# Moving the tiles of a small attention to other SBUF columns, with a new merge of twelve streams of steps

## The chip, the cores and the metric

The kernel runs as one program on one core of a Trainium2 chip, in one launch. Its time is the device time of that core in microseconds (us). The kernel before took 1306.95, 1311.45 and 1311.14 us in three runs; the median is 1311.14 us.

## The reference

Four layers, each an attention and a feed-forward part, over 4 batches of 512 tokens with 128 features. What matters here is layer 0 and its experts, which fill the first third of the span:

```python
# layer 0 attention: 16 heads of 64, 4 key heads, a causal window of 64 tokens
q, k = rmsnorm(q, q_norm_w), rmsnorm(k, k_norm_w)
mask = (i >= j) & (i - j < WIN)
attn = softmax(where(mask, einsum("bhqd,bhkd->bhqk", q, k) / 8, -inf))
y = einsum("bhqk,bhkd->bqhd", attn, v) @ wo.T

# layer 0 feed-forward: a small attention over the 4 batches (at each token
# position, 16 heads of 8), then 8 experts of which each token takes 2
hn = layernorm(x);  q, k, v = split(hn @ in_proj_w.T + in_proj_b)
probs = softmax(where(causal, einsum("sbnd,tbnd->bnst", q, k) / sqrt(8), -inf))
x1 = x + einsum("bnst,tbnd->sbnd", probs, v) @ out_proj_w.T + out_proj_b
hn2 = layernorm(x1);  gates = top2(softmax(hn2 @ router_w.T))
out = x1 + einsum("tef,efh->th", gelu(einsum("th,ehf->tef", hn2, w1)) * gates, w2)
```

Layer 1 has a windowless causal attention (in two halves) and 8 gated experts, layer 2 an attention with 16 heads of 8 and a mixture of low-rank adapters, layer 3 a linear attention and a gated feed-forward.

## The kernel before

The kernel is written for the five engines directly, with semaphores. Its work is cut into 2593 steps. Twelve streams (named a to l) each hold a list of steps in a fixed order: a the layer norms, b the main attention, c the feed-forward, j the mix of layer 0's attention (softmax, transposes, values), l the projections, and so on. The string MERGE, counts and letters, says in which order steps are taken from the streams ("3cl" is three steps of c and one of l). That gives one list of steps for the whole program. Each step has a part on some of the engines, and each engine does its parts in the order of that list, strictly one after the other: a part that waits holds up all that stands behind it on its engine. A step that moves in the merge moves on every engine on which it has a part.

The steps that the change touches or that the prediction speaks of:

- The small attention across batches: `qkv0(b, k)` (ScalarE writes q, k or v of batch b), `bp`, `bs`, `bm`, `be`, `bd`, `bv`, `bo` (products, sums by head, exponentials, weighted sum), `bx` (projection and residual; x1 is left in the tile of k). Its tiles are called qkv; sc0 holds scores.
- Layer 0's attention, for each batch b: `q0(b, p)` and `k0(b, kv)` (projections, copied by VectorE to the arena, L1119 and after), `ks0(b)` (sums of squares, with a power by GpSimd, L1913, whose result TensorE's `kn0(b, kv)` turns), `sc(b, i, x)` (scores on TensorE, maximum by VectorE L1170, four exponentials by ScalarE L1709), `nz` (VectorE divides), `tp(b, i, x)` (transposes on TensorE, L432; copies to pbuf by VectorE L1191 and ScalarE L1721), `yv(b, i)` (values, TensorE), `yt` (L1728), `wo0` (output projection). Queries and keys of the even batches lie in arena columns 0 to 6399, those of the odd batches in columns 9728 to 16127.
- Experts of layer 0: `rts`, `dsp` (the routing), `xt(0, b)` (tokens turned, copied by ScalarE L1747 to tH, and scattered by GpSimd to slots_x in DRAM, 8 indirect DMAs for a batch, L1934). Then 39 blocks of 128 slots in ten groups: `xl(0, q)` (load wA<-slots_x, SyncE L1983; TensorE turns the blocks, L432, VectorE copies to xf, L1328), `up0(q, h)` (TensorE; ScalarE's gelu, L1756, in two halves), `dn0` (TensorE), `stored` (ScalarE's copy tH<-psB, L1764, then the store to slots_y, SyncE L1998), `wl(0, k)` (a block's weights, L1993). `cmb(0, b)` gathers the results from slots_y (GpSimd L1947) when all are stored.

On SyncE's queue the load of a later group (L1983) stands right behind the store of an earlier one (L1998). The tokens of a group sit in one of two buffers, in wA columns 3072 to 4095. The small attention and layer 0's attention share the arena:

```python
qsb = [av[:, o:o + 4096]... for o in (0, 9728)]
kk = [av[:, o + 4096:o + 6400]... for o in (0, 9728)]
qkv = av[:, 9728:15872]...
sc0 = av[:, 15872:18432]...
```

So batch 1's first queries could not be written before the small attention and the layer norm "h2", which reads x1, were done; `q0(1, 0)` waits for them on VectorE (4 waits on ln_xc, one on bo_done).

Of the kernel before, what the change touches and what calls it, by code (L numbers as in the profile page):

```python
# [11 lines left out]
ALU = mybir.AluOpType  # L12
ACT = mybir.ActivationFunctionType
# [38 lines left out]
    "ih3cich2ci2ci2cici5c")
# [108 lines left out]
def build(nc, d, out):  # L161
    ctx = ExitStack()
    with ctx:
# [10 lines left out]
        def cols(t, b):  # L174
            return t[:, b * T:(b + 1) * T]
# [92 lines left out]
        qkv = av[:, 9728:15872].rearrange("p (b a c) -> p b a c", b=4, a=3)  # L268
        sc0 = av[:, 15872:18432].rearrange("p (a c) -> p a c", a=5)
# [144 lines left out]
        def ln_src(tag, b):  # L414
            return qkv[:, b, 1, :] if tag == "h2" else cols(xn if tag == "h1" else xT, b)
# [10 lines left out]
        def tensor(pe):  # L426
# [579 lines left out]
        def vector(dv):  # L1006
# [85 lines left out]
            def bo(s):  # L1092
# [5 lines left out]
                dv.tensor_tensor(qkv[:, s, 0, :], sc0[:, 0, :], sc0[:, 4, :], ALU.mult).then_inc(*bo_done.up(s))  # L1098

            def bx(b):  # L1100
# [3 lines left out]
                dv.scalar_tensor_tensor(qkv[:, b, 1, :], misc("bx", b), vec("outb"), cols(xn, b), ALU.add, ALU.add) \  # L1104
# [3 lines left out]
                add_x(0, b, qkv[:, b, 1, :])  # L1108
# [1268 lines left out]
```

## Time and profile before

| | |
|---|---|
| runs | 1306.95, 1311.45, 1311.14 us; median 1311.14 |
| the profiled execution: time, span | 1302.39 us, 1300.6 us |
| instructions | 23823 |
| granted clock of TensorE, mean | 0.953 |
| busy share of PE, DVE, ACT, POOL | 91%, 69%, 53%, 26% |

PE is TensorE, DVE VectorE, ACT ScalarE, POOL GpSimd, SP and SPq SyncE and its queue. The span runs from the first to the last instruction; the profiled execution's time is 1.8 us longer than its span. A row of a timeline gives the start, the busy time, the engine, the line, the operation with the tile that it writes and those that it reads, the count, and in brackets how long the engine was idle before and what released it. "L428" and "L432" are helpers through which all matmuls and all transposes go, so work is told apart by its tiles and shapes. The clock column gives TensorE's granted clock as a share of full speed. A small change is read where the engine that sets the pace waits, and not from the sums over the span.

### The profile page before, as it was taken

What the parts mean: (1) busy time and instruction counts of PE and PEld (TensorE: products, weight loads), DVE (VectorE), ACT (ScalarE), POOL (GpSimd) and SP (SyncE); (2) the same over time, 40 slices, a digit from 0 to 9 for tenths busy, and PEclk for the clock granted to TensorE, in tenths of its full rate; (3) what the DMA queues carried; (4) which work ended last, traced back from release to release, by engine and by line L of the source; (5) the groups of instructions that cost most, each with busy time, mean ns of one, the idle gap of its engine ahead of it and who ended that gap; (6) DMA issues with size and microseconds to landing.
All of it is one profiled execution on the core that took longest, in us unless ns stands there. A gap on an engine that the chain in (4) does not pass through costs nothing.

```text
span 1300.6 us, 23823 instructions
## 1 busy us (share of the span) xinstructions
PE 1183.6 (91%) x9238; PEld 699.4 (54%) x9238; DVE 900.8 (69%) x1863; ACT 695.3 (53%) x1678; POOL 339.0 (26%) x349
## 2 busy tenths in 40 slices
PE   7957987889888777999999999988999999999998
PEld 4524565756555554566667776744443322334665
DVE  4699754344686688867766777766578887888476
ACT  2455356765864530555555445454666666656621
POOL 1242370000272306722101131075332431111000
PEclk8988888888998895999999999999999999999999
DMA  7200114441110300442433346321404413001000
GB/s 235 61 1 1 58 48 124 113 131 50 39 36 18 98 4 33 131 143 70 133 104 93 111 140 188 108 62 27 104 3 99 102 26 76 3 2 31 1 9 25
DMA packets 71468, 92.41 MB, mean 71 GB/s; under 512 B 9846, under 2 KB 55670, under 8 KB 69766
## 3 DMA queue, kind: packets, MB, share of 16 engines
q1 hardware_dynamic: 67260, 82.50, 22.5%
q0 software_dynamic: 4096, 8.40, 2.1%
q8 instruction: 73, 1.20, 0.4%
q14 instruction: 39, 0.32, 0.1%
HBM read 62.10 MB, written 28.77 MB: 70 GB/s over the span
## 4 chain that ended last, share of the span: by engine, by line
PE 74%; DVE 12%; POOL 5%; ACT 4%; issue 3%; DMA 2%; SPq 0%; DVEq 0%; ACTq 0%
PE psB L428 37%; PE psA L428 30%; PE psB L432 5%; POOL slots_x L1934 2%; DVE mx L1462 2%; POOL tH L1947 2%; PE psA L432 2%; ACT pbuf L1795 1%; DMA wA<-slots_x 1%; DVE st L1170 1%; DVE pbuf L1183 1%; DVE arena L1090 1%; ACT pbuf L1709 1%; DVE st L1173 0%; DVE pbuf L1191 0%
## 5 line engine op out<-in xcount | busy, mean ns | idle before, releaser
L1795 ACT ACTIVATE pbuf<-psA 128x512 f32<-128x512 f32 (+3 forms) x768 | 351.1, 489 | 218.0 <-PE psA L428 211.4
L1462 DVE TENSOR_REDUCE mx<-psA 128x1 f32<-128x512 f32 (+3 forms) x520 | 326.1, 660 | 76.8 <-PE psA L428 74.0
L428 PE MATMUL psA<-arena 64*64 64x128 f32 (+6 forms) x1504 | 152.8, 292 | 3.9 <-DVE mx L1462 1.6
L1709 ACT ACTIVATE pbuf<-psA,st,rq 128x128 f32<-128x128 f32 x256 | 113.5, 459 | 66.4 <-DVE st L1173 66.0
L428 PE MATMUL psB<-pbuf,arena 128*64 128x128 f32 (+4 forms) x1536 | 130.7, 388 | 12.8 <-ACT pbuf L1721 12.2
L428 PEld LDWEIGHTS psA<-arena 64*64 64x64 f32 (+3 forms) x1504 | 83.7, 137 | 62.6 <-ACT pbuf L1795 33.3
L428 PE MATMUL psA<-arena,w 96*128 96x512 bf16 (+4 forms) x320 | 112.7, 410 | 1.3 <-ACT pbuf L1721 1.0
L428 PE MATMUL psA<-w_mdiagT,w_identb 128*128 128x128 bf16 x512 | 108.8, 220 | 0.0
L1851 POOL CAST arena<-tF 16x512 bf16<-16x512 f32 (+2 forms) x24 | 14.5, 605 | 318.2 <-DVE tF L1471 245.8
L428 PE MATMUL psB<-xf,wA 128*128 128x128 f32 x624 | 93.2, 294 | 0.3 <-DVE xf L1328 0.3
L428 PEld LDWEIGHTS psB<-xf,wA 128*128 128x128 f32 x624 | 81.9, 204 | 6.4 <-issue 2.0
L428 PE MATMUL psA<-w,arena 102*128 102x512 bf16 (+5 forms) x272 | 82.6, 338 | 1.3 <-ACT pbuf L1795 0.9
L1893 POOL TENSOR_TENSOR sm<-sm,w_ohalf 128x4 f32<-128x4 f32 x24 | 24.4, 1024 | 210.0 <-DVE sm L1054 209.9
L1947 POOL DMA_INDIRECT tH<-slots_y,slot_i x64 | 63.8, 997 | 57.0 <-DMA slots_y<-tH 37.7
L1934 POOL DMA_INDIRECT slots_x<-tH,slot_i x64 | 62.2, 972 | 51.2 <-ACT tH L1747 19.6
L428 PE MATMUL psA<-w_identb,w_mdiagT 128*128 128x128 bf16 x384 | 73.6, 219 | 0.0
L428 PEld LDWEIGHTS psB<-pbuf,arena 128*5 128x5 f32 (+1 forms) x1536 | 44.8, 106 | 49.8 <-issue 29.3
L428 PE MATMUL psB<-pbuf,res 128*9 128x512 f32 x512 | 66.8, 595 | 0.0
L432 PE MATMUL psA<-w_ident,pbuf 128*128 128x128 f32 x272 | 47.5, 302 | 19.1 <-DVE pbuf L1191 16.2
L428 PE MATMUL psA<-wide,arena 102*128 102x512 bf16 (+4 forms) x192 | 58.8, 330 | 4.4 <-ACT pbuf L1795 3.5
L428 PEld LDWEIGHTS psA<-arena,w 96*128 96x128 bf16 (+1 forms) x320 | 38.3, 123 | 45.5 <-issue 21.4
L1170 DVE TENSOR_REDUCE st<-psA 128x4 f32<-128x512 f32 x64 | 43.6, 682 | 25.9 <-PE psA L428 25.8
(317 smaller groups left out, 2253.4 us busy)
## 6 DMA issues: line engine op xcount, KB each, us to landing
wA<-in_moe SPq DMA_DIRECT2D x39, 576.0 KB, 3.8
wA<-in_moe SPq DMA_DIRECT2D x39, 256.0 KB, 2.9
slots_x<-wA SPq DMA_DIRECT2D x20, 256.0 KB, 3.7
slots_y<-tH SPq DMA_DIRECT2D x18, 256.0 KB, 3.7
wA<-slots_x SPq DMA_DIRECT2D x15, 256.0 KB, 4.0
arena<-stack1k SPq DMA_DIRECT2D x4, 768.0 KB, 7.3
arena<-stack2k SPq DMA_DIRECT2D x8, 384.0 KB, 7.3
stack1q<-arena SPq DMA_DIRECT2D x4, 384.0 KB, 3.5
```

What stands on the lines that cost most here:

```text
L428: return pe.matmul(out, lhsT, rhs, start=start, stop=stop, skip_group_check=True)
L432: return pe.transpose(out, in_, ident[0:n, 0:n])
L1090: dv.reciprocal(sc0[:, 4, :], sc0[:, 4, :]).then_inc(*vstep.up())
L1170: dv.tensor_reduce(mx_, sb0("S", *u).rearrange("p (k c) -> p k c", k=4), AX.X, ALU.max).then_inc(*s_max.up(*u))
L1183: dv.tensor_tensor(Sm(*u), Sm(*u), rcp(*u).unsqueeze(2).to_broadcast([P, 4, P]), ALU.mult).then_inc(*s_n.up(*u))
L1462: dv.tensor_reduce(m[:, t, h:h + c], maxb(lay, b, n)("mx", lay, b, n)[:, 0:c * k].rearrange("p (c k) -> p c k", c=c), AX.X, ALU.max) \
L1709: a = ac.activation(sm[:, k, :], S[:, P * k:P * k + P], ACT.Exp, bias=st[:, 4 + k:5 + k], scale=rq(b)[:, 4 * h + k, kv, x:x + 1], accum_ou ...
L1795: ac.activation(pb(lay, b, s, j)[:, 0:T - q0_], scoreb("ex", lay, b, s, j)[:, 0:T - q0_], ACT.Exp, bias=0.0, scale=1.0) \
L1851: po.tensor_copy(part[0:rows, 0, :], src).then_inc(*pstep.up())
L1893: po.tensor_tensor(st[:, 4:8], st[:, 0:4], W["ohalf"][:, 0:4], ALU.pow).then_inc(*ln_pow.up(tag, b))
L1934: po.indirect_dma_start(Xs[lay], IndirectOffsetOnAxis(i, 0), tok[:, t * P:(t + 1) * P], None) \
L1947: po.indirect_dma_start(tH(*u)[:, t * P:(t + 1) * P], None, Ys[lay], IndirectOffsetOnAxis(i, 0)) \
```

## The change

Two things change. The tiles of the small attention lie elsewhere: q of all batches and k of batches 0 to 2 in wA columns 0 to 3583, k of batch 3 in arena columns 8752 to 9263, the v's in arena columns 16384 to 18431, sc0 in arena columns 13824 to 16383. Arena columns 9728 to 13823, the odd batches' queries, are then untouched by it. The waits that stood before batch 1's first query now stand, with the memset of the keys' pad, before its first key. And the merge string is another one throughout. No arithmetic is changed; the step lists of the streams are the same.

```diff
 MERGE = (
-    "12aca2lcl2c2lcl2c2l3clcl2c2lcl2clcl4cl2cl3cl2clclc2lcb3cb2cjb2cjcbjbcjbj2cj2c2j2c5j2cbc3jcb2cb3cbcjc"
...
+    "11ala2cal2clc2l3clc2l2cl2clclclcl2cl4cl3cl2cl2c2lclc2lb5cbcjcjcb2jbc2bcjcj2cjc2jc3jcjcjlcbcbjbcjcjcj"
...
-        qkv = av[:, 9728:15872].rearrange("p (b a c) -> p b a c", b=4, a=3)
-        sc0 = av[:, 15872:18432].rearrange("p (a c) -> p a c", a=5)
+        sc0 = av[:, 13824:16384].rearrange("p (a c) -> p a c", a=5)
+        kvq = [wA[:, T * k:T * k + T] for k in range(7)] + [av[:, 8752:9264]]
+        qkv = [[kvq[b], kvq[4 + b], av[:, 16384 + T * b:16896 + T * b]] for b in range(NB)]
...
             def q0(b, p):
                 if b > 1:
                     dv.wait_ge(*wo_mm.at(b - 2, p // 4))
-                if b == 1 and p == 0:
-                    for t in range(4):
-                        dv.wait_ge(*ln_xc.at("h2", t))
-                    dv.wait_ge(*bo_done.at(3))
-                    dv.memset(kk[1][:, :, 0:64], 0.0).then_inc(*zeroed1.up())
                 dv.wait_ge(*q_mm.at(b, p))
...
             def k0(b, kv):
                 if b > 1:
                     dv.wait_ge(*s_mm.at(b - 2, 2 * kv + 1))
+                if (b, kv) == (1, 0):
+                    dv.wait_ge(*bo_done.at(3))
+                    dv.wait_ge(*bx_mm.at(0))
+                    dv.memset(kk[1][:, :, 0:64], 0.0).then_inc(*zeroed1.up())
                 dv.wait_ge(*(zeroed1 if b % 2 else zeroed).at())
```

The other edits only name the same tiles in the new way (`qkv[b][k]` for `qkv[:, b, k, :]`) in ln_src, bx, bo, qkv0, bp and bv. Lines between 268 and 1095 of the changed kernel stand one further down than before (L428 is L429, L432 is L433), and the copy of the queries, L1119, is L1115.

In the merged list `q0(1, 0)` stands at place 103 where it stood at 127; `q0(1, 1)` stands at 148 (147 before), `q0(1, 7)` at 162 (163), `k0(1, 0)` at 165 (164), `dsp(0)` at 150 in both.

What the merge does to the engines is shown at three places. GpSimd, where tokens are scattered to the experts' slots (x8 are the eight indirect DMAs of a batch, sq0 the power of `ks0(1)`); before:

```order
L1934 DMA slots_x0<-tH0,slot_i0 5120x128 x8
L1934 DMA slots_x0<-tH1,slot_i0 5120x128 x8
L1913 TENSOR_TENSOR sq0<-sq0,w_ohalf 128x16
L1934 DMA slots_x0<-tH2,slot_i0 5120x128 x8
L1934 DMA slots_x0<-tH3,slot_i0 5120x128 x8
L1913 TENSOR_TENSOR sq0<-sq0,w_ohalf 128x16
```


and with the change:

```order
L1934 DMA slots_x0<-tH0,slot_i0 5120x128 x8
L1934 DMA slots_x0<-tH1,slot_i0 5120x128 x8
L1934 DMA slots_x0<-tH2,slot_i0 5120x128 x8
L1913 TENSOR_TENSOR sq0<-sq0,w_ohalf 128x16
L1934 DMA slots_x0<-tH3,slot_i0 5120x128 x8
L1913 TENSOR_TENSOR sq0<-sq0,w_ohalf 128x16
```


The power has moved behind the third batch's scatters.

ScalarE in the experts' second and third group of blocks (L1756 gelu, L1709 exponentials, L1764 the copy whose store the next load stands behind); before:

```order
L1709 ACTIVATE pbuf,st25<-psA1,st25,rq1 128x128 x4
L1756 ACT_TABLE_LOAD
L1756 ACTIVATE tH4<-psB1 128x512
L1756 ACTIVATE tH5<-psB2 128x512
L1728 ACTIVATE arena<-psB0 128x512
L1683 ACTIVATE wide0<-arena 128x512
L1721 ACTIVATE pbuf<-psA1 128x512
L1764 ACTIVATE tH0<-psB3 128x512
L1709 ACT_TABLE_LOAD
L1709 ACTIVATE pbuf,st20<-psA0,st20,rq1 128x128 x4
L1709 ACTIVATE pbuf,st21<-psA0,st21,rq1 128x128 x4
```


and with the change:

```order
L1683 ACTIVATE wide0<-arena 128x512
L1764 ACTIVATE tH3<-psB3 128x512
L1756 ACT_TABLE_LOAD
L1756 ACTIVATE tH4<-psB2 128x512
L1756 ACTIVATE tH5<-psB1 128x512
L1709 ACT_TABLE_LOAD
L1709 ACTIVATE pbuf,st25<-psA1,st25,rq1 128x128 x4
L1683 ACTIVATE wide0<-arena 128x512
L1728 ACTIVATE arena<-psB0 128x512
L1721 ACTIVATE pbuf<-psA1 128x512
L1764 ACTIVATE tH0<-psB3 128x512
L1709 ACTIVATE pbuf,st20<-psA0,st20,rq1 128x128 x4
```


The table load and one set of four exponentials have moved from behind the copy L1764 to between the gelus and the copy.

TensorE around the first group of blocks (wA turned to psB is `xl(0, 0)`, psA1<-arena,w0 is `wo0(0, 1)`, half of batch 0's output projection, wA,tH4 and wA,tH5 are `dn0`); before:

```order
L428 MATMUL psB0<-pbuf,arena 64x2x64 x8
L428 MATMUL psA0<-arena,w_identb 64x512 x4
L428 MATMUL psA0<-arena 64x128 x16
L428 MATMUL psA1<-arena,w0 128x512 x4
L432 MATMUL psB1<-w_ident,wA 128x128 x4
L432 MATMUL psB2<-w_ident,wA 128x128 x4
L428 MATMUL psB1<-xf0,wA 128x128 x4
L428 MATMUL psB2<-xf0,wA 128x128 x4
L428 MATMUL psB3<-wA,tH4 128x128 x4
L428 MATMUL psB3<-wA,tH5 128x128 x4
L432 MATMUL psA1<-w_ident,pbuf 128x128 x4
```


and with the change:

```order
L433 MATMUL psB1<-w_ident,wA 128x128 x4
L429 MATMUL psB0<-pbuf,arena 64x2x64 x8
L433 MATMUL psB2<-w_ident,wA 128x128 x4
L429 MATMUL psB1<-xf0,wA 128x128 x4
L429 MATMUL psA0<-arena,w_identb 64x512 x4
L429 MATMUL psA0<-arena 64x128 x16
L429 MATMUL psB2<-xf0,wA 128x128 x4
L429 MATMUL psB3<-wA,tH4 128x128 x4
L429 MATMUL psA1<-arena,w0 128x512 x4
L429 MATMUL psB3<-wA,tH5 128x128 x4
L433 MATMUL psA1<-w_ident,pbuf 128x128 x8
```


A set of scores, a step of values and one output projection have moved from ahead of `xl(0, 0)` to behind it, into the group's own chain.

## Rows read from the trace of the kernel before

**Rows 1.** profile page, section 1: busy us of each engine

```profile
PE 1183.6 (91%) x9238; PEld 699.4 (54%) x9238; DVE 900.8 (69%) x1863; ACT 695.3 (53%) x1678; POOL 339.0 (26%) x349
```

**Rows 2.** busy time and clock by stretch (PE, PEld, DVE, ACT, POOL, clock, DMA)

```profile
100.00:125.00 25.00, 17.30 (x155) 8.95 (x146) 24.26 (x39) 12.65 (x41) 4.94 (x4) 0.86 0.00 1
173.00:199.00 26.00, 22.42 (x183) 15.24 (x184) 12.09 (x31) 16.83 (x57) 17.06 (x17) 0.81 0.19 61
...
530.00:850.00 320.00, 317.23 (x2975) 216.21 (x2974) 233.61 (x467) 169.50 (x401) 65.44 (x73) 1.00 0.40 118
```

**Rows 3.** TensorE waits from 60 to 330 us: total us, times, longest us

```profile
PE psB L428 <- ACT pbuf L1721: 9.3, 3, 4.3
...
PE psB L432 <- DMA wA<-slots_x: 7.6, 4, 2.6
PE psA L428 <- ACT pbuf L1709: 7.2, 3, 2.8
```

**Rows 4.** timeline of VectorE: the copy of q0(1, 0)

```profile
127.67 0.69 DVE L1119 COPY arena<-psB 128x512 f32<-128x512 f32 x1 [0.43 <-PE psB L428]
```

**Rows 5.** timeline of GpSimd from 150 to 195 us

```profile
151.24 1.22 POOL L1934 DMA_INDIRECT slots_x<-tH,slot_i  x1 [19.64 <-ACT tH L1747]
...
171.55 2.95 POOL L1913 TENSOR_TENSOR sq<-sq,w_ohalf 128x16 f32<-128x16 f32 x1
...
193.86 0.95 POOL L1934 DMA_INDIRECT slots_x<-tH,slot_i  x1 [0.30 <-issue]
```

**Rows 6.** timeline of TensorE from 174 to 214 us

```profile
174.64 1.09 PE L432 MATMUL psB<-w_ident,sq 128*128 128x128 f32 x4 [0.67 <-POOL sq L1913]
...
188.87 1.09 PE L428 MATMUL psB<-pbuf,arena 128*64 128x128 f32 x16
...
192.11 1.04 PE L428 MATMUL psA<-arena 64*64 64x128 f32 x32
193.08 5.40 PE L428 MATMUL psA<-arena,w 128*128 128x512 f32 x8
198.88 1.44 PE L432 MATMUL psB<-w_ident,wA 128*128 128x128 f32 x8 [0.41 <-DMA wA<-slots_x]
...
211.66 1.97 PE L428 MATMUL psB<-pbuf,arena 128*64 128x128 f32 x16 [3.78 <-ACT pbuf L1721]
213.56 1.11 PE L432 MATMUL psB<-w_ident,wA 128*128 128x128 f32 x4
```

**Rows 7.** timeline of ScalarE in the experts' third group of blocks

```profile
216.47 1.28 ACT L1756 ACT_TABLE_LOAD   x1 [3.10 <-PE psB L428]
217.76 1.08 ACT L1756 ACTIVATE tH<-psB 128x512 f32<-128x512 f32 x2
...
221.54 0.60 ACT L1721 ACTIVATE pbuf<-psA 128x512 f32<-128x512 f32 x1 [2.21 <-PE psA L432]
222.04 0.59 ACT L1764 ACTIVATE tH<-psB 128x512 f32<-128x512 f32 x1
...
225.07 0.46 ACT L1709 ACTIVATE pbuf<-psA,st,rq 128x128 f32<-128x128 f32 x1
...
226.82 0.46 ACT L1709 ACTIVATE pbuf<-psA,st,rq 128x128 f32<-128x128 f32 x1
```

**Rows 8.** timeline of SyncE's queue: the load behind that group's store

```profile
223.08 1.09 SPq L1983 DMA_DIRECT2D wA<-slots_x  x1
```

**Rows 9.** timeline of TensorE: two stalls, at 276 and 318 us

```profile
276.15 1.98 PE L428 MATMUL psB<-pbuf,arena 128*64 128x128 f32 x16 [4.25 <-ACT pbuf L1721]
...
318.20 0.41 PE L428 MATMUL psA<-arena,w_identb 64*64 64x512 bf16 x4 [2.82 <-ACT pbuf L1709]
```

**Rows 10.** timeline of ScalarE: the last copy to tH

```profile
335.11 0.49 ACT L1764 ACTIVATE tH<-psB 128x384 f32<-128x384 f32 x1 [1.05 <-PE psB L428]
```

**Rows 11.** timeline of GpSimd: the first gather

```profile
338.50 1.03 POOL L1947 DMA_INDIRECT tH<-slots_y,slot_i  x1 [37.72 <-DMA slots_y<-tH]
```

**Rows 12.** timeline of TensorE: a wait of tp(3, 2, 1)

```profile
431.98 1.03 PE L432 MATMUL psA<-w_ident,pbuf 128*128 128x128 f32 x4 [2.99 <-DVE pbuf L1191]
```

More of the change, by code:

```diff
@@ new lines @@
+    "2cj2cbj4c2jcj2cjcj2cbcjcj3cjlbjcj2c2lb2jlj5lcj2lbl2jlj2cjl2clbjl3j2lbljcjl2jcljbcbjcjcbcbcj2cj2cjcjc"
+    "2jb2jbcjcjc2j2cbl2cj3cj5cbcjl2c3j2cjbj4cjcjcblcjc2jcjcjbj6cbjcj3cb3cjb2c3jljcj2cj2cljb2j6cj4cb2jlj2l"
+    "2j3ljlc2lcj2clcjlcl2cl2c2lj2lbcb2j2cjcj2cbjcbcjb2cblcjcjcjlbljljljl2jl2jblbjlcla2jljl2jabl2jl2j2bjlj"
+    "ljbab3jljljlbj2l2jc2jb3jc5jljajcj2b2jb2djbjd2jbjbdjajdbjd2jb3jd3jb2jb2ja2jb3jd2j2bjb2ja2jcje2jbe3jec"
+    "2jbeaj2ejejejae2j2ejejej2eaec2ea3ea2ecec2e2c13ec7ec3ed6edec4ebdbc2bebebdbecbk2bdb2ebekbkd2be2bebebkc"
@@ new lines @@
+    "b2ebkbk2e2becbebe2b2kbdcb2e2bcebke2bcde2be2kbecbebebcb2e2bkbebebk2bedbdb2ekbcbebekbebckbecekcb2ebcbd"
+    "bcb2ebcbkebekebcecebcbk2e2bdbeb2kbdbcbe2bebkbe2bekbcbcbebece2bekbcek2bcek2bcebebcbcebkbkbdbebebkbebk"
+    "bde2be2b2kbe2bebebk2edbecbe2bkebc2bk2ebcbk2b2e2bd2ec2be2k2be2kbeb2cb2cebkebek2ebkebcbekbcb2ebc2bkbec"
+    "2bec2bcekbecebcbkekebcbece2cebcebcbek2bkc2bececbce2bdkebe2bkbke2be3ce2be2cb2k2c2ebcbeb2ce2beckbc2b2e"
+    "k2bce2bkcbecec2bkb2ecbebkebecb2ecbkbebkebdbekbc2bebce2bkbebcbebkbe2b2e3cebeckbckebcec2b2eke2b2cbebek"
@@ new lines @@
+    "beb2cecebcbceb2k2b2e2bekebeckb2ecbcbeb2ckcbc2e3cbcbeb2ebkbebcebckdcebkecbcecbecbebebkbdbe2bebkcbdbeb"
+    "ekecece2beck2eckcbcbke3ce2bkcebcbekbc2eck2cbececekebe2bebe2bk2bebcke2bc2ec2bcecebekekbdece2cbe3cbecb"
+    "ebkbebecekc2edbc2becbcbk2ececbe2beke2bekb2ebk2becebcebceb2cecbkek2cbecebeckce2be2cecebcbc2ekbecebeb2"
+    "cebcbecebkcece2ckbc2e2ce2b2cebcbekeb2ekbebe3bke2bebkbe4bekbe2bkeb2ebekb2e2beb2ke3be2bekeb3ebebe4bke2"
+    "be2kbe2bebe2bkbckbebe2beka2ekbe2bk2bc4bk2bcbk4bkbcabkbkbabebckebd2k2bd2bk2ba2bckbkba2bkcebdebc2bkebe"
@@ new lines @@
+    "2bdbk2bkbe2bebkbebkbebkbe2be2bebekbebk2be2bekebebkebebk2bebebkbebe2ba2bkbebekbdebdbkbebk2b2ebcbkbebe"
+    "2bkbebebke2bekb2ebcbkb2ebk2bebebebk2bebebk2e2bkebdbebekbebed2bekbe2be2b2kbebekbebeae2bekebe3b2e2bk2b"
+    "e2be2ke2b2k2bebabekebeab2kbeba2e2bekbebekbebebebdbebeked2bek2bek2bekb2ebab2ebd2b2ekebekbebekbebdbebd"
+    "ke2bdebebkbebebebebkbebebkbebebeke2beke2b3e2bekebaebk2ebdb2e2bkebekebek2b2ekb2ebk2bedebkbebebebebek2"
+    "b2ebekb2ebkbebebkb2e2bekbebebkbebebebe2b2ek2ecebebkbebekb2ebaebebk2e2bkbebebekebebe2bekebebckedbdbeb"
@@ L55 @@
+    "ekebebebebebebekebekb2ebke2beke2bekebekb2ebcbek2e2bebeb2ekbebebebebkbebekbebekebecb2e2bek2becbebkeba"
+    "ebebkbebekebebckbebeb2e2bkbebeabebekebkb2ebebkbebebab2ekebekbebebecbebeabekb2ebk2e2bkebebkea2bkcebek"
+    "e2bekcec2bfbekbce2bcebkbebekbebgbk2be2gbcb2fcbkfbf2bk2bfgbkbfk2bfafbk2bcba2bf2bkbf2bgbkbck2bgbcbgbkb"
+    "gbkbk2bgbg2bgfbkbagkfhck2hckgkhfaghahafghigfcichchichcihci2cicicich2cihchcicih2cih5ci2ci2ci2ci2c")
 class Semaphore:
@@ L1103, in bx @@
                 dv.wait_ge(*ln_done.at("n0", b))
-                dv.scalar_tensor_tensor(qkv[:, b, 1, :], misc("bx", b), vec("outb"), cols(xn, b), ALU.add, ALU.add) \
+                dv.scalar_tensor_tensor(qkv[b][1], misc("bx", b), vec("outb"), cols(xn, b), ALU.add, ALU.add) \
                     .then_inc(*x1_done.up(b))
@@ L1107, in bx @@
                 dv.wait_ge(*x1_done.now())
-                add_x(0, b, qkv[:, b, 1, :])
+                add_x(0, b, qkv[b][1])
             def q0(b, p):
@@ L1661, in qkv0 @@
                 ac.wait_ge(*qkv_mm.at(b, k))
-                ac.activation(qkv[:, b, k, :], misc("qkv", b, k), ACT.Identity, bias=vec(f"inb{k}"), scale=1.0) \
+                ac.activation(qkv[b][k], misc("qkv", b, k), ACT.Identity, bias=vec(f"inb{k}"), scale=1.0) \
                     .then_inc(*qkv_sb.up(b, k))
```

34 lines of the change are left out of this document (5 added, 29 removed).

## The prediction

> **What bounds the kernel.** I read the page first, then a table by stretch, then the waits of the engine that it names, and last timelines at the places where the order changes. TensorE is busy 1183.6 of 1300.6 us [rows 1]; the reader is to see that at most 117 us can be won by any order, and that DVE (900.8) and ACT (695.3) are far from full on average. By stretch it differs: from 530 to 850 us TensorE is busy 317.23 of 320 at full clock, so a new order there can hardly help or hurt; from 100 to 125 us VectorE is busy 24.26 of 25 and TensorE 17.30, so VectorE is the bound; from 173 to 199 us TensorE is busy 22.42 of 26 at clock 0.81 [rows 2]. Between 60 and 330 us its waits come from ScalarE's copy L1721 (9.3 us), ScalarE's exponentials L1709 (7.2 us) and the load wA<-slots_x (7.6 us in 4 times) [rows 3]: the experts' groups are a loop through TensorE, ScalarE and a DMA, and what stands in that loop is paid in full.
>
> **Part 1, the layout.** No instruction is added or removed and no tile changes its size, so the moved columns cost nothing by themselves. The wait that leaves q0(1, 0) lets it go earlier. But the new merge uses this for one step alone: q0(1, 0) goes from place 127 to 103, q0(1, 1) stays at 148. Its copy by VectorE takes 0.69 us and the engine was idle 0.43 us before it [rows 4], and TensorE's late matmuls, not the wait that is removed, released it. In the VectorE-bound stretch the same sets of steps are done before dsp(0), at place 150 in both. One maximum and its product (0.9 us, as long as the 0.69 us copy and a small operation) now stand behind the routing. I take −0.9 us at the first scatter; the bounds are 0 and −1.1 (with the 0.43 us filled, less the 0.27 us of memset that stays anyway).
>
> **Part 2, GpSimd's power.** The scatters start at 151.24, and 16 of them end at 171.5, 1.27 us each; then the power takes 2.95 us and TensorE, which waits 0.67 us for it, goes on at 174.64; the last scatter starts at 193.86 [rows 5, 6]. In the new order the power stands behind 24 scatters: 151.2 − 0.9 + 24 × 1.27 = 180.8, done at 183.8. TensorE arrived at 173.97 and so waits some 10 us. Behind the waiting transpose are queued all keys' norms, the scores of batch 1 and then xl(0, 0). From 174.64 to 198.88 TensorE had 21.3 us of work beside 2.9 us of waits. Of this the merge moves a set of scores (1.3 us with its mask), a step of values (1.0) and wo0(0, 1) (5.4) behind xl(0, 0): 7.7 us [rows 6]. What is left, 13.6 us, ends at about 197.6 to 198.5; the scatters are done 0.9 us earlier than before, so the load lands at about 197.9. So xl(0, 0) comes at 198.9 as before, at best at 198. The 10 us wait is hidden by the scatters, which bound this stretch anyway; but the cover was made of the 7.7 us, and these are now in the experts' loop.
>
> **Part 3, the first group.** Before, TensorE took from 198.88 to 213.56 from the first to the third load, 14.7 us, with a wait of 3.78 us for L1721 before yv(1, 0) [rows 6]. Now the projection stands between the two halves of dn0. I add 7.7, take off the 3.8 us wait (ScalarE has time to catch up while the projection runs), and add 1.7 for ScalarE, which now alternates gelu, exponentials, gelu, exponentials, with two more table loads of 1.28 us each and four exponentials, partly under the projection: +5.6 us. Bounds: +2 (the projection falls wholly under ScalarE's chain) and +9.4 (the wait stays as well).
>
> **Part 4, the exponentials ahead of the copy.** In the third group the gelus start at 217.76, the copy L1764 at 222.04 after an idle time of 2.21 us, and the table load and the exponentials follow it, in the shadow of the transfer: the load is issued at 223.08, and TensorE waits for it, up to 2.6 us [rows 3, 7, 8]. In the new order a table load (1.28) and four exponentials (1.75, from 225.07 to 226.82; with the last one's accumulator 1.87) stand between gelus and copy: 3.15 us. This is so in the second to the sixth group, ahead of the load each time. What the exponentials take of ScalarE's idle time is free: between nothing and 2.21 us. So each costs 0.9 to 3.15 us, and since the exponentials also need scores that TensorE issues late in the group, I take a value above the middle, 2.1 us, in four groups: +8.3. The sixth group holds a 4.25 us wait for L1721 [rows 9] that the same exponentials cause before, and there I add 0. With Part 3 this makes +13.9 at the load of the eighth group.
>
> The row shows the gelu 1.29 us after the table load begins, so a switch costs 1.28 us [rows 7]. The Trainium skill (*ScalarE: Activation LUTs*, What ACT_TABLE_LOAD costs) has 1283 ns and a drain of some 1380 ns, 2.66 us for a switch. The trace agrees with the first and shows no second between the load and the gelu; had it been paid, four groups would be 5.5 us dearer. [...]
>
> **Part 5, the end of the experts.** The wait of 2.82 us for exponentials at 318.20 [rows 9] goes, since they come earlier: −2.8. The last copy, at 335.11, after 1.05 us of idle time, now has a table load and exponentials ahead of it, and the gathers start at 338.50, after its store [rows 10, 11]. +3.5; bounds +2.1 (3.15 less the idle 1.05) and +5 (two sets). The gathers (32, to 398) set when layer 1 can begin, so this is not hidden. A wait of 2.99 us of batch 3's transposes for VectorE [rows 12] shrinks, since the step whose copy it waits for stands earlier: −2; bounds 0 and −3. After 530 us I take 0, with 3 us either way: in the next 320 us TensorE has 2.8 us idle [rows 2].
>
> **The sum.** −0.9 + 5.6 + 8.3 − 2.8 + 3.5 − 2 = +11.7, from which I take 1.7 for xl(0, 0), which may come up to 0.9 us sooner, and for waits that absorb a late arrival: +10. The profiled execution took 1302.39 us, so the changed one would take 1312.4. It lies 8.75 us under the median of 1311.14; the runs shown are what the new time is compared with, so I forecast 1311.14 + 10 = 1321 us.
>
> **Rivals.** A measurement of this kernel can tell about 0.5% (6.6 us) from no change; the bounds are 1304.6 and 1317.7.
>
> *Rival A, faster: the stalls behind exponentials are what is paid, and the new order removes them.* The waits of 3.78, 4.25 and 2.82 us [rows 6, 9] and the 2 us later on make 12.9 us. They are won if a group's copy L1764 ends no later than before, relative to its load, that is, if the 3.15 us fit into ScalarE's idle time and the transfer's shadow; the idle 2.21 us [rows 7] speaks for two thirds of it. It decides from about 8 us from load to copy. Then parts 3 and 4 fall to 2 + 3, and 5 + 3.5 − 12.9 − 0.9 − 2 (after 530 us) = −7: 1304. Against: in the groups the TensorE waits for the load, not for ScalarE, in 4 of them.
>
> *Rival B, about the same: the loop has room.* TensorE idles about a fifth of each group; the moved 7.7 us fall into these holes, and a part of the exponentials too: 2 + 4 × 0.9 − 2.8 + 3.5 − 2 − 0.9 = +3.4, or 1314.5.
>
> *Rival C, slower by more: the clock.* TensorE's granted clock is 0.81 from 173 to 199 us [rows 2], that is, part of the stretch at 1.2 GHz, half of full speed. If the wait of 10 us is followed by a stretch at half clock that is as long as that wait or longer, the 13.6 us behind it stretch by up to half of the length, +5, and xl(0, 0) comes late; with the groups at the upper bound (4 × 3.15 instead of 8.3, +4.3) that gives +19: 1330.
>
> *Rival D: the change does not do what it says.* By the order it holds in part, since one query block alone uses the freed columns; with the rest of the merge left as it is in the forecast, its price is the 0.9 us of part 1, and the time would be 1322.
>
> **How the numbers follow.** The forecast 45%, its own range 1315 to 1328. Rival A 20%, rival B 24%, rival C 11%. The new string was merged anew over all 2593 steps, and I weighed only those places in which an order changes on an engine that waits; sums of small gains elsewhere would help A and B, hence their weight. The range for 8 in 10 reaches from 1301 (A with 3 us more won after 530 us) to 1330 (C). Slower than 1317.7: three quarters of the forecast, all of C and a little of B: 48%. Within: the rest of the forecast, most of B and some of A: 30%. Faster than 1304.6: the larger part of A and some of B: 22%.
>
> **What would show it.** In the profile of the changed kernel: GpSimd's power at about 181 behind 24 scatters and a TensorE wait for it of 9 to 12 us (part 2 is wrong if it is under 5); xl(0, 0) at 198 to 199; the third load's transposes 5 us later than 213.56, and the eighth group's some 14 us later than 278.96 minus what the start won (parts 3 and 4 are wrong if it is under 6); a table load between gelu and copy in the second to the sixth group; 23 table loads; no wait of 2.8 us for exponentials near 320; the first gather 12 to 15 us later than 338.50. The forecast as a whole is wrong if the first gather comes within 4 us of 338.50, or if the stretch from there to the end changes by more than 5 us.

## The result: slower by 1.7%, twice the forecast

The changed kernel took 1330.48, 1331.94, 1325.97 and 1332.36 us, median 1331.21; the kernel before took 1309.05 us (median of four). The ratio is 1.0166, 95% interval 1.0124 to 1.0207: slower by 22 us, where I had forecast 10, with 1330 as the upper end. The profiled execution took 1330.48 us (span 1328.6), 28 us more than that of before; of these, 6.7 us are the distance of before's profiled execution from its own median.

The page of the changed kernel, the lines that answer to [rows 1]: busy us by engine, TensorE's granted clock in 40 slices, and the shares of the chain by engine.

```profile
PE 1190.7 (90%) x9238; PEld 703.1 (53%) x9238; DVE 899.4 (68%) x1863; ACT 699.3 (53%) x1682; POOL 338.6 (25%) x349
...
PEclk8888879889989896899999999999999999999999
...
PE 65%; DVE 12%; ACT 9%; POOL 6%; DMA 4%; issue 3%; SPq 1%; ACTq 0%; POOLq 0%; DVEq 0%
```

TensorE's work is the same; its idle time grows from 117 to 138 us, and its busy time by 7 us, in part because more of it runs at half clock (granted clock 0.953 before, 0.947 here). That is 21 + 7 = 28. By stretch (us of PE, PEld, DVE, ACT, POOL busy, clock, DMA), against [rows 2]:

```profile
178.00:204.00 26.00, 14.63 (x120) 10.87 (x118) 10.54 (x26) 7.90 (x24) 17.94 (x16) 0.75 0.16 52
520.00:550.00 30.00, 24.92 (x139) 12.84 (x137) 20.34 (x42) 7.67 (x15) 23.84 (x26) 0.80 0.34 109
545.00:865.00 320.00, 313.42 (x2891) 211.99 (x2891) 227.70 (x465) 161.67 (x386) 64.49 (x71) 0.99 0.40 119
```

From 178 to 204 us TensorE is busy 14.63 us where it was 22.42. From 545 to 865, the stretch that I had left at 0, it is busy 313.42 of 320 us where it was 317.23.

GpSimd and TensorE at the power (start, us, engine, line, operation; in brackets the idle time before and its releaser), against [rows 5, 6]:

```profile
156.30 1.22 POOL L1934 DMA_INDIRECT slots_x<-tH,slot_i  x1 [20.34 <-ACT tH L1747]
...
187.35 2.94 POOL L1913 TENSOR_TENSOR sq<-sq,w_ohalf 128x16 f32<-128x16 f32 x1
...
199.45 0.96 POOL L1934 DMA_INDIRECT slots_x<-tH,slot_i  x1 [0.30 <-issue]
...
357.70 1.03 POOL L1947 DMA_INDIRECT tH<-slots_y,slot_i  x1 [38.56 <-DMA slots_y<-tH]
```

```profile
190.43 1.94 PE L433 MATMUL psB<-w_ident,sq 128*128 128x128 f32 x8 [10.16 <-POOL sq L1913]
...
205.45 0.66 PE L433 MATMUL psB<-w_ident,wA 128*128 128x128 f32 x4
...
213.59 3.60 PE L429 MATMUL psA<-arena,w 128*128 128x512 f32 x8
217.69 1.16 PE L429 MATMUL psB<-wA,tH 128*128 128x128 f32 x8 [0.50 <-ACT tH L1756]
...
224.81 0.66 PE L433 MATMUL psB<-w_ident,wA 128*128 128x128 f32 x4 [1.63 <-DMA wA<-slots_x]
...
238.69 1.11 PE L433 MATMUL psB<-w_ident,wA 128*128 128x128 f32 x4 [4.47 <-DMA wA<-slots_x]
```

The power stands behind 24 scatters and TensorE waits 10.16 us for it. The first load's turn is at 205.45, 49.2 us behind the first scatter (47.6 before). The projection, 3.60 us, stands between the halves of `dn0`, and the third load's turn comes at 224.81: 68.5 us behind the first scatter, where it was 62.3. The same eight matmuls took 5.40 us before [rows 6]; the granted clock was 0.68 from 193.10 to 198.50 us there and 1.00 from 213.60 to 217.20 here.

ScalarE in the group behind the third load, against [rows 7]:

```profile
226.88 1.28 ACT L1756 ACT_TABLE_LOAD   x1
228.17 0.60 ACT L1756 ACTIVATE tH<-psB 128x512 f32<-128x512 f32 x1
...
229.14 0.60 ACT L1756 ACTIVATE tH<-psB 128x512 f32<-128x512 f32 x1
...
230.26 1.28 ACT L1709 ACT_TABLE_LOAD   x1
232.26 0.46 ACT L1709 ACTIVATE pbuf<-psA,st,rq 128x128 f32<-128x128 f32 x1 [0.72 <-DVE st L1173]
...
234.54 0.60 ACT L1764 ACTIVATE tH<-psB 128x512 f32<-128x512 f32 x1
```

A table load and four exponentials stand between gelu and copy, as the order said. The whole trace has 23 table loads (19 before). The gelu starts 1.29 us behind the start of its table load; a switch costs 1.28 us here too, and the drain of the Trainium skill (*ScalarE: Activation LUTs*, What ACT_TABLE_LOAD costs) does not show. TensorE's waits from the first load to the first gather (us in total, times, longest), of the kernel before and then of the changed one; the two stretches are 139 and 152 us long:

```profile
PE psB L428 <- ACT pbuf L1721: 8.0, 2, 4.3
PE psB L432 <- DMA wA<-slots_x: 7.2, 3, 2.6
PE psA L428 <- ACT pbuf L1709: 2.8, 1, 2.8
PE psB L428 <- ACT tH L1756: 1.1, 2, 0.8
```

```profile
PE psB L429 <- ACT tH L1756: 11.5, 7, 3.5
PE psB L433 <- DMA wA<-slots_x: 11.2, 6, 4.5
PE psB L429 <- ACT pbuf L1721: 3.4, 3, 2.4
PE psA L429 <- ACT pbuf L1709: 1.5, 1, 1.5
```

The stalls behind L1721 are gone (8.0 to 3.4), and in their place TensorE waits for gelus (1.1 to 11.5) and loads (7.2 to 11.2).

**Where the 28 us are.** At many places of the merge both orders have done exactly the same set of steps. The time at which TensorE has finished such a set can be read from the timeline of any kernel with either order, and cuts the span into stretches that can be compared. Length of each stretch in us, TensorE's idle time (length less busy time) behind the slash; the last one ends with TensorE's last matmul, 3.3 us ahead of the span's end:

```
steps         before      changed    changed, run again   new from 624 on
0-42       49.0/ 7.2    52.8/ 7.3       49.1/ 7.1         47.4/ 7.5  (old order)
42-151     99.2/25.5    99.5/25.8      101.6/26.8         98.1/25.9  (old order)
151-223    57.0/ 6.4    67.2/17.5       66.7/14.7         57.0/ 8.1  (old order)
223-425   151.0/22.9   155.7/29.8      154.6/31.4        147.1/24.2  (old order)
425-624   158.4/33.2   152.8/30.6      154.9/30.3        160.8/31.4  (old order)
624-743    47.0/ 2.6    52.0/ 3.4       51.9/ 3.4         50.2/ 5.6
743-1316  209.5/ 0.9   213.6/ 3.3      212.6/ 2.5        212.0/ 2.1
1316-1422  37.8/ 0.0    42.0/ 2.4       42.2/ 2.6         40.9/ 2.9
1422-1649  92.1/ 8.9    89.5/ 6.7       89.3/ 6.5         89.3/ 6.6
1649-2346 256.2/ 4.5   259.6/ 5.8      259.7/ 5.8        259.6/ 5.9
2346-2593 140.0/ 1.5   140.7/ 2.0      145.3/ 2.0        140.6/ 2.0
```

In the changed kernel's trace that is +4.1 us up to step 151, +14.9 from there to 425, −5.6 from 425 to 624, and +14.8 behind. The first row as windows, of the kernel before and of the changed one, with the granted clock behind the five engines:

```profile
0.00:48.97 48.97, 41.77 (x178) 24.69 (x180) 24.61 (x52) 15.93 (x24) 9.74 (x13) 0.93 0.67 196
```

```profile
0.00:52.84 52.84, 45.55 (x177) 26.14 (x178) 24.70 (x51) 16.43 (x25) 8.20 (x12) 0.87 0.63 182
```

Step 151 is the routing `dsp(0)`, 223 the end of the first group of blocks, 425 the start of layer 1, 624 to 743 the start of its experts, 1649 its end. Behind 743 the length of some stretches is nearly a property of the order: 743 to 1316 took 209.5 us in eight of eleven profiled executions with the old order (209.8 twice and 211.1 in the others) and 212.0 to 213.6 in all nine with the new.

### The profile page after: what moved, and what is told of

It is laid out like the page before. It is cut to its first block, busy times and chain, and to the rows that moved or that the text cites. A ratio compares the mean times of both kernels' runs of the same rounds, so it can differ in the third digit from the quotient of the medians.

```text
span 1328.6 us, 23844 instructions
## 1 busy us (share of the span) xinstructions
PE 1190.7 (90%) x9238; PEld 703.1 (53%) x9238; DVE 899.4 (68%) x1863; ACT 699.3 (53%) x1682; POOL 338.6 (25%) x349
## 4 chain that ended last, share of the span: by engine, by line
PE 65%; DVE 12%; ACT 9%; POOL 6%; DMA 4%; issue 3%; SPq 1%; ACTq 0%; POOLq 0%; DVEq 0%
PE psB L429 32%; PE psA L429 27%; PE psB L433 5%; ACT pbuf L1709 4%; POOL slots_x L1934 2%; POOL tH L1947 2%; DVE mx L1462 2%; PE psA L433 2%; DVE st L1170 1%; DMA wA<-slots_x 1%; ACT pbuf L1795 1%; DVE pbuf L1183 1%; ACT L1756 1%; DVE st L1173 1%; DVE xT L1026 1%
## 5 line engine op out<-in xcount | busy, mean ns | idle before, releaser
L1709 ACT ACTIVATE pbuf<-psA,st,rq 128x128 f32<-128x128 f32 x256 | 113.8, 460 | 89.9 <-DVE st L1173 88.0
L429 PE MATMUL psA<-arena 64*64 64x128 f32 (+7 forms) x1504 | 156.3, 294 | 3.7 <-ACT pbuf L1795 1.0
L429 PE MATMUL psB<-pbuf,arena 128*64 128x128 f32 (+4 forms) x1536 | 133.0, 395 | 6.9 <-ACT pbuf L1721 6.0
L429 PEld LDWEIGHTS psA<-arena 64*64 64x64 f32 (+3 forms) x1504 | 84.5, 139 | 65.3 <-ACT pbuf L1795 30.3
L429 PE MATMUL psA<-arena,w 96*128 96x512 bf16 (+4 forms) x320 | 110.0, 394 | 1.9 <-ACT pbuf L1721 1.5
L429 PE MATMUL psA<-w_mdiagT,w_identb 128*128 128x128 bf16 x512 | 110.1, 221 | 0.0
L429 PE MATMUL psB<-xf,wA 128*128 128x128 f32 x624 | 92.3, 291 | 2.2 <-DMA wA<-in_moe 2.1
L429 PEld LDWEIGHTS psB<-xf,wA 128*128 128x128 f32 x624 | 80.7, 201 | 9.6 <-issue 5.5
L429 PE MATMUL psA<-w,arena 102*128 102x512 bf16 (+5 forms) x272 | 83.4, 338 | 2.2 <-DMA w<-scr1m 1.3
L429 PE MATMUL psA<-w_identb,w_mdiagT 128*128 128x128 bf16 x384 | 74.0, 220 | 0.0
L429 PEld LDWEIGHTS psB<-pbuf,arena 128*5 128x5 f32 (+1 forms) x1536 | 47.2, 108 | 45.0 <-issue 24.9
L429 PE MATMUL psB<-pbuf,res 128*9 128x512 f32 x512 | 66.9, 595 | 0.1
L429 PE MATMUL psB<-wA,tH 128*128 128x128 f32 x390 | 57.7, 290 | 8.0 <-ACT tH L1756 8.0
L429 PE MATMUL psA<-wide,arena 102*128 102x512 bf16 (+4 forms) x192 | 60.6, 331 | 3.1 <-ACT pbuf L1795 1.8
L433 PE MATMUL psA<-w_ident,pbuf 128*128 128x128 f32 x272 | 48.8, 308 | 13.9 <-DVE pbuf L1191 11.3
```

What stands on the lines that cost most here:

```text
L429: return pe.matmul(out, lhsT, rhs, start=start, stop=stop, skip_group_check=True)
L433: return pe.transpose(out, in_, ident[0:n, 0:n])
L1709: a = ac.activation(sm[:, k, :], S[:, P * k:P * k + P], ACT.Exp, bias=st[:, 4 + k:5 + k], scale=rq(b)[:, 4 * h + k, kv, x:x + 1], accum_ou ...
```

## The experiments

All kernels below have the changed tiles and waits; "old" and "new" are the step lists of the two merges, cut only where both have done the same set. A ratio is over the kernel before on the same chip, with its 95% interval. The six groups of runs (the changed kernel's first four count as one) are of two kinds: in three of them the kernel before takes 1304 to 1309 us, in the other three 1412 to 1416, and there most effects drown; the last section shows where the time goes. The kind is named with each result. An interval is 0.2 to 0.4% wide to either side, 3 to 5 us, so a difference of two runs below some 5 us is not sure by the runs alone.

**1. The layout alone, and single stretches (the 1416 us kind).**

```diff
-order = new[0:2593]
+order = old[0:2593]                                    # layout_old_merge
+order = new[0:149] + old[149:2593]                     # new_to_149
+order = old[0:149] + new[149:421] + old[421:2593]      # new_149_to_421
+order = old[0:421] + new[421:2593]                     # new_from_421
```

> The changed tiles and waits with the merge string of before. If all of the loss comes from the order (my theory), the time is that of before within 3 us. If the places of the tiles cost something by themselves (rival), it is 5 us or more above before; had the freed wait a value of its own, it would be below before by up to 1 us.

Measured 0.9975 (0.9947 to 1.0003). The tiles' places cost nothing. Whether layout and removed wait bring a microsecond or two the interval leaves open.

> The changed layout, the new order for the first 149 steps (the small attention and the start of layer 0's attention), the old one behind. After 149 steps both orders have done the same set of steps. Theory, by the two traces (GpSimd's first scatter at 156.3 instead of 151.2 us): +5 us to the end, since the scatters set when the experts begin. Rival: the 5 us are taken up later by waits (the scatters hide nothing of TensorE's work), +0 to 2 us. My prediction had put -0.9 here.

Measured 0.9989 (0.9969 to 1.0008): none of the +5 us is seen here.

> The new order for steps 150 to 421 alone (scatters, experts of layer 0, batches 1 and 2 of its attention). Theory, the sum of parts 2 to 5 of the prediction: first gather 14 us later than 338.5, the time +10 to +14 us. Rival: the experts' part is cheaper without the late start, under +6 us, and the rest of the loss comes from elsewhere.

Measured 0.9989 (0.9965 to 1.0012): 0, against +10 to +14.

> The old order up to step 421, the new one behind (layers 1 to 3 and the last batch of layer 0's attention). The two traces differ by 9 to 12 us in what follows the first gather. Theory: this is the order's own, +5 to +9 us, with TensorE's half clock at 530 and 544 us seen here too. Rival: it is a consequence of the late start or differs from run to run, then 0 to 2 us. My prediction had put -2 and 0 here.

Measured 1.0055 (1.0020 to 1.0090): +8 us. So in this group the only stretch whose price was seen at all was the one for which I had taken −2 and 0. On the 1305 us kind the order's stretches were asked for again, from the other side.

**2. Leaving stretches out of the changed kernel (1304.61 us before).**

```diff
+order = new[0:2593]                                    # after_again
+order = new[0:149] + old[149:421] + new[421:2593]      # new_but_old_149_to_421
+order = new[0:421] + old[421:2593]                     # new_to_421
```

> The changed kernel once more, beside the kernel before, on the chip that this group of runs gets. The kernel before took 1309 us in its first runs and 1416 us on the chip of the previous group, where none of the three single stretches of the new order added more than 0.8%. Theory (the loss is the order's own, wherever it runs): ratio 1.012 to 1.02 on this chip. Rival (what the order costs depends on the chip: where the engines stall for other reasons the new order hides them as well): 1.003 to 1.010.

Measured 1333.52 us, 1.0226 (1.0191 to 1.0262): +28.9.

> The new order, but the steps from 149 to 421 (scatters, experts of layer 0) in the old one. Theory: this takes away parts 2 to 5 of the prediction, 10 to 14 us of the changed kernel's loss, and leaves 8 to 12. Rival: the experts' stretch hides it, under 5 us are taken away.

Measured 1316.70 us, 1.0111 (1.0078 to 1.0144): +12.1. The experts' stretch carries 16.8 us of the changed kernel's 28.9.

> The new order for the first 421 steps, the old one behind. Theory: early part and experts together, +14 to +17 us, and the rest of the changed kernel's loss (5 to 8 us) comes from what is left out here. Rival (the later stretches repay nothing and cost nothing): as much as the changed kernel, +22.

Measured 1322.93 us, 1.0139 (1.0107 to 1.0171): +18.3. What lies behind step 421 carries 10.6 us. What is left, 28.9 − 16.8 − 10.6 = 1.5 us, is that of the first 149 steps, within the noise.

**3. The exponentials behind the copy.** In the changed kernel, in the second to the sixth group:

```diff
-xl.0.3 ... up0.2.1 dn0.2.0 sc.1.3.1 ... dn0.2.1 ... st.0.2
+xl.0.3 ... up0.2.1 dn0.2.0 ...          dn0.2.1 ... st.0.2 sc.1.3.1
```

> The new order, but in the second to the sixth group of the experts' blocks the step of scores that stands between gelu and copy is moved behind the copy (with one division and one step of values in the fourth group). The table load and the exponentials are in the shadow of the transfer again. Theory (part 4): 6 to 10 us less than the changed kernel. Rival (ScalarE's idle time and the transfers take the exponentials anyway): 0 to 3 us less. By the rule of the Trainium skill (ScalarE: Activation LUTs, What ACT_TABLE_LOAD costs), with a drain at each switch, it would be up to 11 us.

Measured 1333.82 us, 1.0230 (1.0199 to 1.0262), beside 1.0226 for the changed kernel in the same group: nothing. TensorE's waits from the first load to the first gather, of the changed kernel run again and of this one:

```profile
PE psB L429 <- ACT tH L1756: 11.9, 7, 3.5
PE psB L433 <- DMA wA<-slots_x: 10.9, 5, 4.6
```

```profile
PE psB L429 <- ACT tH L1756: 16.2, 9, 3.5
PE psB L433 <- DMA wA<-slots_x: 11.9, 6, 3.2
```

TensorE now waits longer for gelus (16.2 us instead of 11.9) and no less for loads. Counted from the first load, this kernel is 2.7 us ahead of the other at the fifth group's first matmuls, level at the eighth's and 4.3 us behind at the ninth's. My theory for part 4 falls in its cause: its size is right (below), but moving the step of scores behind the copy does not take it away. A step moves on every engine, so its matmuls went with the exponentials; ScalarE's part alone was not tested.

**4. GpSimd's power, and the work ahead of the first load (1304.12 us before).**

```diff
-q0.1.7 k0.1.0 k0.1.1 xt.0.2 yt.0.4 k0.1.2 k0.1.3 sc.0.6.1 ks0.1
+q0.1.7 k0.1.0 k0.1.1 yt.0.4 k0.1.2 k0.1.3 sc.0.6.1 ks0.1 xt.0.2   # power_ahead_of_third_scatters

+order = new[0:149] + old[149:223] + new[223:2593]      # new_but_old_149_to_223
```

> The changed kernel, with the step xt(0, 2) (turning, copy and scatters of batch 2's tokens) moved behind ks0(1), so that GpSimd's power stands behind 16 scatters again. Theory (part 2 of the prediction): TensorE's wait of 10 us for the power goes, but it comes back as a wait for the first load, since the scatters set that; time within 2 us of the changed kernel. Rival (the wait is paid in full): 8 to 10 us less.

Measured 1327.95 us, 1.0187 (1.0149 to 1.0224), +23.8. The changed kernel did not run in this group; it had 1.0166 and 1.0226 (+22.2 and +28.9) in two others, and this lies between, so the wait is not paid in full. TensorE of this kernel, at the keys' norm and at the first load:

```profile
176.34 1.08 PE L433 MATMUL psB<-w_ident,sq 128*128 128x128 f32 x8 [0.27 <-POOL sq L1913]
...
202.11 1.11 PE L433 MATMUL psB<-w_ident,wA 128*128 128x128 f32 x4 [12.40 <-DMA wA<-slots_x]
```

The wait for the power is 0.27 us, and 12.40 us of waiting stand before the load. From the first scatter to the first load's turn it is 49.2 us with the power in either place (152.94 to 202.11 here; 48.6 in the changed kernel run again). So the 10 us wait was hidden, as part 2 said.

> The new order with steps 149 to 223 (scatters, power, the work ahead of the first load, the first group of blocks) in the old one. Theory (part 3): the first group is short again, 5 to 8 us less than the changed kernel. Rival, if the groups behind absorb it: under 3 us less.

Measured 1320.60 us, 1.0117 (1.0083 to 1.0151): +16.5, which is 6 us less than the changed kernel's +22.2 and 12 us less than its +28.9, both of other groups. The first agrees with the theory, the second is more; the runs don't decide. In the traces, first scatter to first gather takes 194.9 us here, 201.2 and 201.4 in the changed kernel, 187.3 in the kernel before. That is 6.4 us for part 3.

**5. Behind step 421, in parts.**

```diff
+order = old[0:421] + new[421:624] + old[624:2593]      # new_421_to_624
+order = old[0:624] + new[624:2593]                     # new_624_to_end
+order = old[0:624] + new[624:743] + old[743:2593]      # new_624_to_743 and _again
+order = old[0:743] + new[743:1649] + old[1649:2593]    # new_743_to_1649
+order = old[0:1649] + new[1649:2593]                   # new_from_1649
```

> The changed layout, the old order, with steps 421 to 624 alone in the new one. In four profiled executions with the new order this stretch was 1.7 to 5.7 us shorter than in the kernel before. Theory: the gain is the order's own; 3 to 5 us below before, faster than both kernels. Rival (the stretch was shorter only because what came in was late and waits were absorbed): within 1.5 us of before.

Measured 1301.51 us (ten runs) against 1304.12: 0.9970 (0.9951 to 0.9988). This version beats both kernels, that of before by 2.6 us and the changed one by 25 to 32 us. The stretch of steps 425 to 624, as one row of windows:

```profile
355.90:510.45 154.55, 123.42 (x1151) 85.08 (x1150) 118.04 (x268) 66.28 (x229) 58.31 (x56) 0.86 0.13 38
```

154.55 us, where it took 158.40 before. In the other six traces of the 1305 us kind with this stretch in the new order it took 152.8 to 157.0 us, in the other two with the old order 160.8 and 164.9. The changed tiles are in this kernel too, and they alone measured 0.9975 on the other kind, so the runs alone don't tell order from layout. The trace does: up to step 425 it agrees with that of before to 0.3 us (355.90 and 356.21), so the layout brings nothing there.

> The changed layout, the old order to step 624, the new one from there to the end, the stretch for which the prediction took 0. In the four profiled executions with the new order it was 15 to 18.6 us longer than in the kernel before, and 3.4 longer where only what lay ahead of it was new. Theory: +11 to +16 us over before, from the order behind 624 alone. Rival (knock-on of the late start and of the clock that falls behind it): under +5 us.

Measured 1317.70 us, 1.0098 (1.0063 to 1.0133): +13.6 by the medians, +12.8 by the ratio. Steps 743 to 1316 and 1649 to 2346 as windows, of the kernel before and then of this one:

```profile
561.60:771.11 209.51, 208.63 (x1940) 142.36 (x1938) 150.82 (x314) 114.17 (x268) 41.47 (x45) 1.00 0.36 104
...
901.03:1157.20 256.17, 251.65 (x1603) 96.44 (x1604) 195.95 (x381) 166.57 (x341) 74.19 (x83) 1.00 0.23 53
```

```profile
560.57:772.54 211.97, 209.89 (x1939) 142.39 (x1938) 151.22 (x314) 113.55 (x269) 38.03 (x44) 1.00 0.34 103
...
902.83:1162.46 259.63, 253.75 (x1599) 97.21 (x1598) 197.29 (x383) 167.18 (x340) 75.03 (x84) 1.00 0.23 52
```

At full clock throughout, the first stretch is 2.5 us longer with 1.3 us more of busy time, the second 3.5 us longer with 2.1 more. About half of the loss is TensorE being busy for longer with the same steps, in another order. Why a step takes longer there is open.

> The changed layout, the old order, steps 624 to 743 alone in the new one (the start of layer 1's experts). By the traces: +3 to +5 us. Theory (one place): half of the late loss or more is here, +5 to +8. Rival (spread): +2 to +4.

Measured 1.0005 (0.9973 to 1.0037), on the 1412 us kind.

> The same with steps 743 to 1649 (the rest of layer 1). By the traces 3 + 2.7 - 2.5 = +3.2 us. Theory (one place, elsewhere): 0 to +2. Rival (spread): +3 to +5, with a TensorE wait of 2 to 3 us for a load of the experts' weights and a short fall of the clock behind it.

Measured 1.0041 (1.0009 to 1.0073): +5.8 us, same kind.

> The same with all steps from 1649 on (layers 2 and 3). By the traces +3.4 us up to step 2346, in which TensorE's idle time grows by 1 us only, and 0 behind. Theory (spread): +3 to +4. Rival (the differences of the traces are those of single executions): within 1.5 us of before.

Measured 1.0015 (0.9988 to 1.0041): +2.1 us, same kind. Its steps 1649 to 2346 took 259.4 us, those of the old order 256.2 on both kinds.

> The changed layout, the old order, steps 624 to 743 in the new one, once more, for a chip on which the kernel before takes 1305 to 1310 us. Theory (the late loss is spread): +2 to +5 us. Rival (it sits here): +6 us or more. On a chip where the kernel before takes 1412 us, 0 again.

Measured 0.9997 (0.9959 to 1.0035), once more on the 1413 us kind, so this one stretch's price without the halts was not timed; the table has it at +3.2 to +5.0. By the traces the late loss is spread: no part of it carries more than half. By the runs alone, with some 4 us either way on each part, that is not sure.

**6. The freed columns, used as the change uses them.**

```diff
-yv.0.1 bm.3 be.3 sc.0.3.0 bd.3 ... ln2.h2.1 q0.1.0 yt.0.2
+yv.0.1 bm.3 be.3 q0.1.0 sc.0.3.0 bd.3 ... ln2.h2.1 yt.0.2
```

> The old order, in which only q0(1, 0) is moved, from place 127 to 102, behind be(3), as the freed columns allow. Theory (part 1 of the prediction: VectorE bounds this stretch, and the step's 0.69 us copy now stands in the chain of the small attention): -0.5 to +1.5 us. Rival (TensorE's idle time there takes the step, and the stretch behind is shorter by its 1.1 us): -1 to -2 us.

Measured 1.0038 (1.0008 to 1.0067), on the 1412 us kind.

> The old order with q0(1, 0) alone moved forward, once more. Theory: VectorE and the small attention's chain bound the stretch, so the step costs there what it takes (its copy of 0.69 us, TensorE's 1.1 us): 0 to +2 us. Rival: the +4 us of the last group are its real price. Second rival: a gain of 1 to 2 us.

Measured 1.0001 (0.9964 to 1.0039), the same kind. No gain in either; whether it costs 1 us or nothing these runs can't tell. Both traces have steps 42 to 151 at 100.7 us, a little above the old order's range of 98.1 to 100.3.

## Why the prediction was wrong, step by step

- **Part 1 (−0.9 us): wrong in sign, by the traces.** Steps 42 to 151 took 99.5 to 101.6 us in eight profiled executions with the new order (mean 100.4) and 98.1 to 100.3 in ten with the old (mean 99.3). The first 42 steps, which I had not weighed at all, took 50.3 us on average (47.9 to 52.8) against 48.3 (46.5 to 49.6). Together some +3 us in place of −0.9; by the runs it is 1.5 us or nothing. The first 42 steps follow the granted clock. At a clock of 0.93 both orders take 48.9 to 49.6 us. Four of the eight traces with the new order lie below it, at 0.87 to 0.90, and none with the old. Whether the order brings that clock or chance does is open.
- **Part 2 (a 10 us wait that is hidden): right,** shown by the 12.40 us that take its place. The load still came at 205.45 and not at 198 to 199: 5.1 us of that are the later first scatter, 1.5 us a longer way from scatter to load.
- **Part 3 (+5.6 us in the first group, from a scatter 0.9 us early, so +6.5 from scatter to third load): right.** Measured +6.2 and +5.5. From the first to the third load alone it is 19.4 and 19.2 us against 14.7, +4.7 and +4.5. One term of the sum was too large: the projection was taken at 5.4 us, its time at a clock of 0.68, and took 3.60 at full clock.
- **Part 4 and the first half of part 5 (+8.3 − 2.8 + 3.5 = +9.0 from the third load to the first gather): right in size.** Measured +8.0 and +8.5 in two executions, 7.1 with the old order up to step 223. That is against the 124.9 us of before; two other traces with the old order there have 120.9 and 121.5, so it may be up to 12. The cause that I gave for part 4 is not shown: moving the scores and their exponentials behind the copy gave nothing.
- **"Waits of batch 3's transposes shrink, −2":** right in sign, too small. Steps 425 to 624 took 5.6 and 3.5 us less, and 2.6 us of that are there as time when the stretch is new alone.
- **"After 530 us I take 0, with 3 us either way": this step failed.** Measured +14.8 us from step 624 to the end in the changed kernel's trace, +10.1 in the trace and 13 by the runs where the old order runs up to 624. I argued that in a stretch where TensorE is busy 99% of the time at full clock a new order can hardly help or hurt. The row shows only that it can't help much: a bound engine leaves little to win, and says nothing of what can be lost. In the changed kernel the loss is 3 to 5 us in each of four stretches, and made of several things: waits for a load of weights and for other engines (5.2 us more idle time behind step 624), steps that take longer one by one, and half clocks. The clock fell again at 529 to 535, 546 to 549 and 819 to 822 us, where before it stayed at full behind 514; the row of 520 to 550 above has it at 0.80. That is some 14 us at half clock, up to 7 us of time, and in other executions the falls come at other places. They are not needed for the loss: with the old order up to 624 the clock is 1.00 in every stretch behind it, and 10.1 us are lost all the same.

The last sign that I had named for a wrong forecast came true as well: from the first gather (357.70) to the end it takes 8.8 us longer than before, where 5 was the limit.

With 13 in place of 0 and +3 in place of −0.9, less 2 for steps 425 to 624, the sum of the prediction becomes 10 + 13 + 4 − 2 = +25, between the two measurements of the changed kernel (+22 and +29). Rivals A and B needed the idle time of the groups to take up the exponentials, and it did not. Rival C forecast 1330 and came nearest in time, which is luck: its 5 us at the half clock behind the 10 us wait are not there (49.2 us from scatter to load with the wait and without).

## What to carry to other kernels

When an order written out for the whole program is replaced, price every stretch of it: cut both orders where they have done the same set of steps, and compare engine by engine between the cuts, the bound stretches too. A busy share of 99% says how much can be won, not how much can be lost. Such cuts also let single stretches be exchanged, and show a part worth keeping in a change that loses as a whole: here 200 steps of 2593 that gain 0.3%. A time read from a row belongs to the clock of that row: look at the granted clock before it goes into a sum.

## What the runs showed of the hardware

The kernel before took 1304 to 1309 us in three groups of runs and 1412 to 1416 us in three others. The record gives the same chip number to a group of either kind (1304.12 and 1413.17 us), so whether the kind belongs to a chip or to a time is not shown. Of the 104 us between two traces with the old order, 89 lie in three stretches in which GpSimd issues indirect transfers: steps 151 to 223 took 84 us instead of 57, 425 to 624 took 186 instead of 158, and 1422 to 1649 took 126 instead of 92. Steps 743 to 1422 and 1649 to 2346 took the same 209.5 + 37.8 and 256.2 us to a tenth. In the slow stretches several engines stand still without a releaser in the program. VectorE of the changed layout with the old order, while the scatters run:

```profile
157.39 0.69 DVE L1170 TENSOR_REDUCE st<-psA 128x4 f32<-128x512 f32 x1 [5.07 <-remote]
...
171.76 1.29 DVE L1115 COPY arena<-psB 128x512 f32<-128x512 f32 x2 [12.25 <-remote]
```

12.25 us of idle time whose releaser is given as "remote", and TensorE waits for that copy. What the engines wait for there no run shows. It matters for experiments: where such a halt lies, a new order that costs 10 us in a group of one kind does not show in the other (151 to 223: 85.7 us with the new order, 82.7 to 87.1 in seven traces with the old), and the ratio of a whole program says little about its parts.

A second thing: on a bound TensorE at full clock, the length of the 573 steps from 743 to 1316 was the same to 0.1 us in eight of eleven executions, in groups of both kinds. There the trace of one execution resolves effects that 10 timed runs, which spread over 15 us, do not.
